# First attention: row-packed 48-row products for the softmax maxima, with the operand stacks laid out for two heads at once

## The chip, the cores and the metric

One core of a Trainium2 chip runs the whole program. The metric is the device time of one execution in microseconds (us). TensorE (PE) multiplies, VectorE (DVE) reduces and does elementwise work, ScalarE (ACT) does exponentials and copies, GpSimd (POOL) fills and gathers, SyncE (SP) issues DMAs.

## The reference, cut to what matters

A two-layer model over 8 images, each of 384 tokens (256 image rows and 128 text rows) with 256 channels. Only the first attention is touched. It has 16 heads of 16 channels and two sets of keys:

```
q, k, v, kp = heads(xn @ W_Q.T), heads(xn @ W_K.T), heads(xn @ W_V.T), heads(xn @ W_K_prime.T)
out = alpha * softmax(q k^T / 4) v + (1 - alpha) * softmax(q kp^T / 4) v
h = h + out @ W_O.T
```

## The kernel before, in words

`attention0` works image by image. An image's q, k and k' are projected in f32 and each is split into three bf16 parts (`parts`, L704 on ACT, L779, L782 and L784 on DVE), stored to a scratch array in HBM (L479) and read back as stacks of rows (L490): `qs` and `ks` hold, for each head, six blocks of 16 rows, one for each pair of parts in `SLOTS`, 96 rows in all (`NS`). A bf16 product of two stacks is then the sum of six part products. Four more rows in each stack carry the negated row maxima and the ones and zeros that switch them on for the right kind of key, so the scores that go to the exponential have 100 rows.

The 16 heads times 2 kinds of key are 32 units. While the units of image i are scored, the maxima of image i+1 are made:

- `scores` (L596): three matmuls for a unit into PSUM banks 4 to 6, then ACT's exponential over all three (L731). The next unit's scores wait for that exponential.
- `values` (L607): four matmuls of 128 rows by 32 columns, each in its own column quarter, in three of every four units (not in the first of a group of four).
- `ring`: three PSUM banks, one product of 128 x 384 in each (L584), reduced to a column of maxima by DVE (L795). An image has 96 products and, after each half of the heads, one transpose of the maxima (L581), which waits for all reduces so far. DVE negates and splits the maxima (L799, L802) and SP copies them as rows into `qs` (L499). `ring_part(v)` gives unit v three entries (four in two units).
- bank 3 serves one step in most units by the table `BANK3`: transposes of inputs (L545), outputs (L616) and y (L622), projections (L554, L562) and the output product (L630). A step waits until the step before it has been read out of the bank.

Each engine runs its own program in order. In a unit PE runs scores, values, ring entries, the bank-3 step. DVE runs the unit's reduces, then the unit's bank-3 work (three `low_parts` instructions for a projection, `normalize` for outputs, an addition). So a reduce of unit v+1 stands behind the bank-3 work of unit v.

Ahead of the loop lie two parts. A first block loads and transposes weights and makes layer-norm statistics. In the second block GpSimd fills the four switching rows of `ks` by four fills (L535, L538), while DVE normalizes image 0 (L768), PE and DVE make its parts, SP stores and stacks them. Then `first_ring` makes image 0's maxima, mixed with the projections of image 1, and the first scores follow.

SP's order in an image's turn: stacks of the next image's second half of heads, rows of maxima of its first half, the stores of the image after next, its first stacks, rows of maxima of the second half. A half's stacks are 18 DMAs, the maxima of a half 4.

## Time and profile before

| | |
|---|---|
| median of 3 runs | 2127.85 us (2125.75 to 2127.95) |
| the profiled execution | 2124.57 us, span 2122.70 us |
| attention0, first block | about 124.9 to 149.5 us |
| start to the first scores | about 150.0 to 280.8 us |
| the eight images' turns | about 280.8 to 915 us |

The profiled execution's time is 1.87 us over its span and 3.28 us under the median. In the rows below a time is in us from the start of the span unless it says ns, and a row of the timeline merges neighbouring instructions of one line.

### The profile page before, as it was taken

The numbers are of one execution on the slowest core, as the hardware profiler recorded it, in microseconds if no ns is written. First come the engines' busy times: TensorE is split into PE (matmuls) and PEld (weight loads), VectorE is DVE, ScalarE is ACT, GpSimd is POOL, SyncE is SP. The second block draws the span as 40 slices with busy tenths as digits, with TensorE's granted clock in tenths as the row PEclk, the third lists the DMA queues.
The fourth block names the chain that finished last, engine by engine and source line by source line (L and its number), as shares of the span: only waits on it lengthen the run. The fifth ranks groups of instructions, "written<-read, shape, count | busy, mean of one in ns | idle before, by whom it ended". The sixth has DMA issues, their size and how long they took to land. (4 is left out here: it accounts for less than half of the span.)

```text
span 2122.7 us, 29473 instructions
## 1 busy us (share of the span) xinstructions
PE 1828.5 (86%) x10095; PEld 1157.5 (55%) x10095; DVE 1102.2 (52%) x2272; ACT 667.6 (31%) x1032; POOL 352.9 (17%) x287
## 2 busy tenths in 40 slices
PE   5833698898898899758999589999989999999998
PEld 3521233433343343236666355666656676899997
DVE  6556778777787788147776454544332111222221
ACT  0111035564555555634444222323221111011110
POOL 0016000000000000017787021221102221100000
PEclk9876779999999999979999799999999999999999
DMA  4113824354364250010000470000001000334211
GB/s 150 52 47 58 110 34 80 67 58 69 55 82 68 35 96 8 1 46 0 0 0 0 155 253 1 0 0 0 1 1 37 30 25 22 114 140 151 94 36 33
DMA packets 112282, 117.25 MB, mean 55 GB/s; under 512 B 11453, under 2 KB 104127, under 8 KB 111936
## 3 DMA queue, kind: packets, MB, share of 16 engines
q1 hardware_dynamic: 99040, 87.73, 20.0%
q10 hardware_dynamic: 9504, 18.88, 2.5%
q0 software_dynamic: 3648, 9.46, 1.2%
q8 instruction: 54, 0.88, 0.2%
q14 instruction: 36, 0.29, 0.1%
HBM read 80.87 MB, written 35.29 MB: 55 GB/s over the span
## 5 line engine op out<-in xcount | busy, mean ns | idle before, releaser
L795 DVE TENSOR_REDUCE mx<-ps_a 128x1 f32<-128x384 f32 x768 | 375.5, 549 | 86.1 <-PE ps_a L584 83.9
L731 ACT ACTIVATE prob<-ps_a 128x1152 f32<-128x1152 f32 x256 | 289.4, 1130 | 216.0 <-PE ps_a L596 214.7
L584 PE MATMUL ps_a<-ks,qs 96*128 96x384 bf16 x768 | 197.7, 351 | 26.5 <-DMA ks<-parts_dram 17.0
L1820 PEld LDWEIGHTS ps_e<-xTr,w 128*128 128x128 f32 x1792 | 204.4, 192 | 2.2 <-issue 0.8
L1820 PE MATMUL ps_e<-xTr,w 128*128 128x128 f32 x1792 | 204.7, 275 | 0.6 <-DVE xTr L1993 0.6
L596 PE MATMUL ps_a<-qs,ks 100*128 100x384 bf16 x768 | 172.2, 333 | 24.2 <-ACT prob L731 19.8
L1756 PE MATMUL ps_e<-xT_all,w 128*128 (+1 forms) x512 | 169.7, 491 | 0.9 <-ACT xT_all L1847 0.9
L584 PEld LDWEIGHTS ps_a<-ks,qs 96*128 96x128 bf16 x768 | 62.4, 99 | 197.9 <-DVE mx L795 118.5
L607 PE MATMUL ps_a<-prob,vp 128*32 128x384 f32 x1536 | 165.5, 504 | 0.0
L1042 POOL TENSOR_TENSOR xb_f<-xb_f,xm_f 128x256 f32<-128x256 f32 x24 | 18.0, 752 | 755.7 <-ACT xm_f L1154 755.7
L1756 PEld LDWEIGHTS ps_e<-xT_all,w 128*128 128x128 f32 x512 | 97.5, 192 | 66.5 <-issue 1.8
L1090 PE MATMUL ps_f<-wguT,xT_f 128*128 128x352 f32 x384 | 123.2, 465 | 2.5 <-ACT xT_f L1135 2.5
L1883 ACT ACTIVATE gel_r<-ps_e 128x512 f32<-128x512 f32 x56 | 33.4, 597 | 279.9 <-PE ps_e L1820 279.9
L596 PEld LDWEIGHTS ps_a<-qs,ks 100*128 100x128 bf16 x768 | 64.2, 98 | 100.3 <-ACT prob L731 58.2
L1900 DVE TENSOR_TENSOR hid_e<-gel,ps_e 128x384 f32<-128x384 f32 x64 | 35.5, 554 | 136.0 <-ACT gel L1853 121.7
L1829 PE MATMUL ps_e<-w,hid_r 128*128 128x256 f32 x448 | 101.3, 379 | 0.0
L1462 PE MATMUL ps_a<-wsT,xT_a 128*128 128x512 f32 x192 | 88.8, 606 | 10.5 <-DVE lg L1364 10.0
L1853 ACT ACTIVATE gel<-ps_e 128x384 f32<-128x384 f32 x64 | 31.4, 490 | 207.3 <-PE ps_e L1756 207.3
L1090 PEld LDWEIGHTS ps_f<-wguT,xT_f 128*128 128x128 f32 x384 | 71.9, 193 | 36.1 <-ACT xT_f L1135 3.3
L2004 DVE TENSOR_TENSOR hid_r<-gel_r,ps_e 128x512 f32<-128x512 f32 x56 | 38.5, 687 | 100.4 <-ACT gel_r L1883 100.4
L1829 PEld LDWEIGHTS ps_e<-w,hid_r 128*128 128x128 f32 x448 | 82.9, 190 | 10.1
L554 PE MATMUL ps_a<-xT,wT 128*128 128x384 f32 x192 | 76.2, 524 | 14.0 <-DVE parts L784 12.6
(225 smaller groups left out, 2618.6 us busy)
## 6 DMA issues: line engine op xcount, KB each, us to landing
ks<-parts_dram SPq DMA_DIRECT2D x192, 96.0 KB, 6.4
w<-in_L_ffn_W_dram ACTq DMA_DIRECT2D x18, 1024.0 KB, 8.3
parts_dram<-parts SPq DMA_DIRECT2D x24, 576.0 KB, 3.7
qs<-parts_dram SPq DMA_DIRECT2D x96, 96.0 KB, 4.5
pix<-in_x_dram SPq DMA_DIRECT2D x24, 256.0 KB, 4.1
w<-in_L_ffn_W_dram SPq DMA_DIRECT2D x6, 1024.0 KB, 12.0
grouped_x<-empty_row SPq DMA_DIRECT2D x1, 4352.0 KB, 23.9
grouped_h<-empty_row SPq DMA_DIRECT2D x1, 4240.5 KB, 35.6
```

Source lines behind the costliest of these rows:

```text
L554: mm = pe.matmul(ps[:, bank, 0:T], wT[:, m, k, a * P:(a + 1) * P], xT[:, k], start=(k == 0), stop=(k == KC - 1))
L584: mm = pe.matmul(ps[:, r % 3, 0:T], qs[0:NS, b, u // 2, t * P:(t + 1) * P], ks[0:NS, b, u % 2, u // 2], start=True, stop=True)
L596: mm = pe.matmul(ps[:, 4 + t, 0:T], ks[0:NS + 4, b, kp, hh, t * P:(t + 1) * P], qs[0:NS + 4, b, hh], start=True, stop=True)
L607: mm = pe.matmul(ps[j * SLOT:(j + 1) * SLOT, 7, 0:T], vp[:, b, t, g // 2 * QUAD + j], prob[:, g % 2, j, t], start=(t == 0), stop=(t == TT ...
L731: act.activation(prob[:, g % 2, j], ps[:, 4:7, 0:T], ACT.Exp).then_inc(exp_done.sem, 1)
L795: dve.tensor_reduce(at, ps[:, r % 3, 0:T], AX.X, ALU.max).then_inc(ring_free.sem, 1)
L1090: mm = pe.matmul(ps[:, 2 * (u % 2) + n, 0:HALF0], xT[:, t, k], wguT[:, n, k, s * HALF0:(s + 1) * HALF0], start=(k == 0), stop=(k == KC - 1))
L1462: mm = pe.matmul(ps[:, n], xT[:, k, t * P:(t + 1) * P], wsT[:, k, n * 512:(n + 1) * 512], start=(k == 0), stop=(k == KC - 1))
L1756: mm = pe.matmul(ps[:, 2 * (a % 2) + m, 0:T], w12[:, 0, m, k, a * P:(a + 1) * P], xT_all[:, i, k], start=(k == 0), stop=(k == KC - 1))
L1820: mm = pe.matmul(ps[:, 2 * n + m, a * P:(a + 1) * P], w12[:, b, m, k, n * HALF1 + a * P:n * HALF1 + (a + 1) * P], xTr[:, k], start=(k == 0 ...
L1829: mm = pe.matmul(ps[:, 4, 0:C], hid_r[:, a], w3[:, b, a], start=(a == 0), stop=(a == IT1 - 1))
L2004: dve.tensor_tensor(hid_r[:, n * 4:(n + 1) * 4].rearrange("p a t -> p (a t)"), gel_r[:, n], ps[:, 2 * n + 1], ALU.mult).then_inc(rhid_done ...
```

## The change

1. The six part products are divided into `MAIN` (three) and `MINOR` (three). The products for the maxima use only the three main ones, 48 rows. The scores still use all six.
2. The stacks take all 128 rows. A head on side 0 has its main rows at 0 to 47 and its minor rows at 64 to 111, a head on side 1 the other way about. Heads 0 to 3 and 8 to 11 are on side 0, the others on side 1. The switching rows are 48 to 51 or 112 to 115. The scores take rows 0 to 111 or 0 to 115, with zeros between the blocks.
3. A ring item is now a pair: the same query tile and kind for one head of each side, at row offsets 0 and 64 of the array (`tile_position`), in two of the three banks. A pair waits until the item before the last entry is free, which for the second pair of a unit means that the first product of its first pair is reduced.
4. An image has 48 pairs and 2 transposes, 50 items, one or two in a unit (`ring_part`). The first item of a unit stands right behind its scores, ahead of `values`, the second behind `values`. DVE's order is as before: all reduces of a unit, then its bank-3 work. The first ring has two items (four reduces) for each projection step, where it had three reduces.
5. Stacks are one DMA for each block and side: 36 DMAs of 48 KB a half in place of 18 of 96 KB. Rows of maxima: 8 a half in place of 4.
6. The four fills of `ks` on GpSimd in the second block go. GpSimd now fills, in the first block, a small tile `ones` (four short fills) and zeros rows 32 to 63 of `qs` and `ks` as uint32 (6144 and 12288 elements a partition), and SP copies `ones` into the switching rows by 16 DMAs at the head of the second block.

```diff
-SLOTS = ((0, 0), (1, 0), (2, 0), (0, 1), (1, 1), (0, 2))
-NS = len(SLOTS) * D0
+MAIN = ((0, 0), (1, 0), (0, 1))
+MINOR = ((2, 0), (1, 1), (0, 2))
+NS = len(MAIN) * D0
+UPPER = P // 2
...
+    RING = [(q, kp, t) for q in range(QUAD) for kp in range(KINDS) for t in range(TT)] + [None]
+    NI = 2 * len(RING)
+    NT2 = 2 * len(RING) - 1
+    NR = 2 * NT2
     def ring_part(v):
-        return range(NR * v // UNITS, NR * (v + 1) // UNITS)
+        return list(range(NI * v // UNITS, NI * (v + 1) // UNITS))
+    def ring_item(e):
+        half, n = divmod(e, len(RING))
+        return half, n, half * NT2 + 2 * n
...
-    EARLY = 3
+    EARLY = 2
...
+            @block.gpsimd
+            def _(pool):
+                for kp in range(KINDS):
+                    pool.memset(ones[0:4, kp], float(kp)).then_inc(ones_made.sem, 1)
+                pool.wait_ge(ones_made.sem, 2)
+                for kp in range(KINDS):
+                    pool.memset(ones[0:2, kp], 1.0 - kp).then_inc(ones_made.sem, 1)
+                for stack in (qs[UPPER // 2:UPPER].rearrange("p b h t -> p (b h t)"),
+                              ks[UPPER // 2:UPPER].rearrange("p b k h t -> p (b k h t)")):
+                    pool.memset(stack.bitcast(U32), 0).then_inc(rows_zero.sem, 1)
...
-                        for s, pair in enumerate(SLOTS):
+                        for side in range(2):
+                            heads = quad(half, side)
+                            for pair, r in slot_rows(side):
...
+                for b in range(2):
+                    for kp in range(KINDS):
+                        for half in range(2):
+                            for side in range(2):
+                                r = shift_row(side, 0, 0)
+                                sp.dma_start(ks[r:r + 4, b, kp, quad(half, side)],
+                                             ones[:, kp].unsqueeze(1).to_broadcast([4, QUAD, T])).then_inc(ks_ready.sem, 16)
...
-            @block.gpsimd
-            def _(pool):
-                for kp in range(KINDS):
-                    pool.memset(ks[NS:NS + 4, :, kp], float(kp)).then_inc(ks_ready.sem, 1)
-                pool.wait_ge(ks_ready.sem, 2)
-                for kp in range(KINDS):
-                    pool.memset(ks[NS:NS + 2, :, kp], 1.0 - kp).then_inc(ks_ready.sem, 1)
...
+                        if r:
+                            pe.wait_ge(ring_free.sem, ring_free.at(i, r - 1))
...
+                        for side in range(2):
+                            hh, rows = (2 * half + side) * QUAD + q, main_rows(side)
+                            pe.matmul(ps[:, (r + side) % 3, 0:T], qs[rows, b, hh, t * P:(t + 1) * P],
+                                      ks[rows, b, kp, hh], start=True, stop=True, tile_position=(side * UPPER, 0)
+                                      ).then_inc(ring_full.sem, 1)
...
                         scores(i, b, v)
+                        if more:
+                            ring(i + 1, 1 - b, ring_part(v)[:1])
                         if j and g:
                             values(i, b, g - 1, j - 1)
...
                         if more:
-                            ring(i + 1, 1 - b, ring_part(v))
+                            ring(i + 1, 1 - b, ring_part(v)[1:])
```

## Rows read from the trace of the kernel before

**Rows 1.** The page, busy time and share of each engine.
```profile
PE 1828.5 (86%) x10095; PEld 1157.5 (55%) x10095; DVE 1102.2 (52%) x2272; ACT 667.6 (31%) x1032; POOL 352.9 (17%) x287
```
**Rows 2.** Windows: stretch, length, busy time by engine, granted clock, DMA share, GB/s.
```profile
181.40:218.30 36.90, 16.03 (x45) 9.29 (x45) 13.26 (x21) 5.33 (x11) 10.21 (x1) 0.69 0.63 102
218.30:280.70 62.40, 49.14 (x125) 15.44 (x126) 54.30 (x116) 4.70 (x8) 0.00 (x0) 0.69 0.58 82
615.50:698.10 82.60, 74.26 (x471) 32.09 (x471) 65.52 (x151) 44.76 (x52) 0.00 (x0) 1.00 0.44 66
```
**Rows 3.** Timeline of the second block's opening: start, length, instruction.
```profile
150.00 20.76 POOL L535 MEMSET ks<- 4x12288 bf16 x2 [146.73 <-POOLq L405]
150.04 31.29 DVE L768 TENSOR_SCALAR xn<-h,mv,rstd 128x256 f32<-128x256 f32 x3 [0.53 <-PEq L405]
...
187.57 4.25 DVE L782 CAST parts<-rest 128x384 bf16<-128x384 f32 x1
...
192.92 0.36 DVE L782 CAST parts<-rest 128x384 bf16<-128x384 f32 x1
...
199.61 1.05 DVE L768 TENSOR_SCALAR xn<-h,mv,rstd 128x256 f32<-128x256 f32 x3
```
**Rows 4.** Timeline of the first stacks and the first ring product.
```profile
200.12 3.62 SPq L490 DMA_DIRECT2D qs<-parts_dram  x6
203.78 5.63 SPq L490 DMA_DIRECT2D ks<-parts_dram  x12
...
218.35 1.12 PE L584 MATMUL ps_a<-ks,qs 96*128 96x384 bf16 x3 [17.02 <-DMA ks<-parts_dram]
...
218.87 3.09 DVE L795 TENSOR_REDUCE mx<-ps_a 128x1 f32<-128x384 f32 x6 [18.21 <-PE ps_a L584]
```
**Rows 5.** Timeline of the first block, DVE.
```profile
132.01 1.34 DVE L440 MEMSET vp<- 128x1536 f32 x1 [0.27 <-issue]
```
**Rows 6.** Timeline of one unit without a bank-3 step, PE, ACT and DVE.
```profile
514.67 0.66 PE L596 MATMUL ps_a<-qs,ks 100*128 100x384 bf16 x3
...
515.26 0.85 PE L607 MATMUL ps_a<-prob,vp 128*32 128x384 f32 x8
515.37 1.13 ACT L731 ACTIVATE prob<-ps_a 128x1152 f32<-128x1152 f32 x1 [0.76 <-PE ps_a L596]
...
516.05 0.66 PE L584 MATMUL ps_a<-ks,qs 96*128 96x384 bf16 x3
516.42 1.49 DVE L795 TENSOR_REDUCE mx<-ps_a 128x1 f32<-128x384 f32 x3 [0.40 <-PE ps_a L584]
...
516.56 0.66 PE L596 MATMUL ps_a<-qs,ks 100*128 100x384 bf16 x3
```
**Rows 7.** Timeline of units 14 and 15, a projection behind a projection.
```profile
651.86 0.56 DVE L784 TENSOR_TENSOR parts<-rest,parts 128x384 bf16<-128x384 f32 x1
652.34 1.48 DVE L795 TENSOR_REDUCE mx<-ps_a 128x1 f32<-128x384 f32 x3
...
652.48 1.56 PE L554 MATMUL ps_a<-xT,wT 128*128 128x384 f32 x4 [0.29 <-DVE parts L784]
...
653.87 0.65 PE L596 MATMUL ps_a<-qs,ks 100*128 100x384 bf16 x3
...
656.05 1.48 DVE L795 TENSOR_REDUCE mx<-ps_a 128x1 f32<-128x384 f32 x3
657.59 0.12 PEld L581 LDWEIGHTS ps_a<-ident,mx 128*96 128x96 f32 x1 [2.08 <-DVE mx L795]
```
**Rows 8.** Timeline of unit 1, DVE's outputs ahead of its reduces.
```profile
701.41 0.22 DVE L818 RECIPROCAL rec<-ps_a 128x12 f32<-128x12 f32 x1
...
701.93 0.36 DVE L824 TENSOR_TENSOR y<-ps_a,rec 128x192 f32<-128x192 f32 x1
```
**Rows 9.** Timeline, SP's stacks of a first half in a later turn.
```profile
501.25 3.43 SPq L490 DMA_DIRECT2D qs<-parts_dram  x6
...
504.72 7.22 SPq L490 DMA_DIRECT2D ks<-parts_dram  x12
```

More of the change, by code:

```diff
@@ L338, in attention0, with side_of, main_rows, slot_rows @@
     NM = HALF * TT
[L340 to L342 removed]
+    RING = [(q, kp, t) for q in range(QUAD) for kp in range(KINDS) for t in range(TT)] + [None]
+    NI = 2 * len(RING)
+    NT2 = 2 * len(RING) - 1
+    NR = 2 * NT2
     def ring_part(v):
[L346 removed]
+        return list(range(NI * v // UNITS, NI * (v + 1) // UNITS))
+    def ring_item(e):
+        half, n = divmod(e, len(RING))
+        return half, n, half * NT2 + 2 * n
+    def side_of(hh):
+        return hh // QUAD % 2
+    def main_rows(side):
+        return slice(side * UPPER, side * UPPER + NS)
+    def slot_rows(side):
+        for s in range(len(MAIN)):
+            yield MAIN[s], side * UPPER + s * D0
+            yield MINOR[s], (1 - side) * UPPER + s * D0
+    def shift_row(side, kp, k):
+        return side * UPPER + NS + 2 * kp + k
+    def all_rows(side):
+        return slice(0, UPPER + NS + 4 * side)
     BANK3 = {0: ("turn_outputs", 6), 3: ("values", 0), 4: ("turn_outputs", 7), 5: ("values", 1),
@@ L391, in attention0 @@
         mneg = sb("mneg", [P, 2, 2, P], BF16)
+        ones = sb("kind_rows", [4, KINDS, T], BF16)
         prob = sb("prob", [P, 2, QUAD, TT, T])
@@ L493, in maxima @@
                 def maxima(i, b, half):
                     sp.wait_ge(mneg_done.sem, mneg_done.at(i, half + 1))
+                    n = QUAD * TT
                     for kp in range(KINDS):
-                        for k in range(2):
-                            r = NS + 2 * kp + k
-                            n = NM // KINDS
-                            sp.dma_start(qs[r:r + 1, b, half * H0 // 2:(half + 1) * H0 // 2]
-                                         .rearrange("o h (a q) -> o (h a) q", q=P),
-                                         mneg[kp * n:(kp + 1) * n, half, k]).then_inc(mrow_in[half].sem, 16)
+                        for side in range(2):
+                            for k in range(2):
+                                r = shift_row(side, kp, k)
+                                sp.dma_start(qs[r:r + 1, b, quad(half, side)].rearrange("o h (a q) -> o (h a) q", q=P),
+                                             mneg[(2 * kp + side) * n:(2 * kp + side + 1) * n, half, k]
+                                             ).then_inc(mrow_in[half].sem, 16)
@@ L566, in ring @@
                 def ring(i, b, entries):
-                    for r in entries:
-                        u, t = RING[r]
-                        if r in (0, NR // 2):
+                    for e in entries:
+                        half, n, r = ring_item(e)
+                        if n == 0:
                             for m in range(3):
-                                signal = stack_in[r // (NR // 2)][m]
-                                pe.wait_ge(signal.sem, signal.at(i, 16 * len(SLOTS)))
-                        back = 3 if t is not None else 1
-                        if r >= back:
-                            pe.wait_ge(ring_free.sem, ring_free.at(i, r - back + 1))
+                                signal = stack_in[half][m]
+                                pe.wait_ge(signal.sem, signal.at(i, signal.per))
+                        if RING[n] is None:
+                            pe.wait_ge(ring_free.sem, ring_free.at(i, r))
+                            pe.transpose(ps[0:2 * NM, r % 3, 0:P], mx[:, half:half + 2].rearrange("p n k h t -> p (n k h t)"),
+                                         ident[:]).then_inc(ring_full.sem, 1)
+                            continue
+                        if r:
+                            pe.wait_ge(ring_free.sem, ring_free.at(i, r - 1))
@@ L586, in ring @@
-                        mm.then_inc(ring_full.sem, 1)
+                        q, kp, t = RING[n]
+                        for side in range(2):
+                            hh, rows = (2 * half + side) * QUAD + q, main_rows(side)
+                            pe.matmul(ps[:, (r + side) % 3, 0:T], qs[rows, b, hh, t * P:(t + 1) * P],
+                                      ks[rows, b, kp, hh], start=True, stop=True, tile_position=(side * UPPER, 0)
+                                      ).then_inc(ring_full.sem, 1)
```

62 lines of the change are left out of this document (30 added, 32 removed).

## The prediction

> **What bounds the kernel now.** I read the page first. PE is busy 86% of the span and no other engine over 52% [rows 1]. That is an average over five stages, so the share decides nothing here: the change touches the first attention alone, 124.9 to 915 us. I then took windows of its parts. From the start of image 0 (150 us) to the first stack products (218.3 us) hardly anything is computed. In the first ring (62.4 us) DVE is busy 54.3 us at a granted clock of 0.69, between TensorE's two levels. In a full turn of 82.6 us PE is modelled busy 74.3 us and DVE 65.5 us at clock 1.00, so neither is full [rows 2]. The timeline tells who waits. In the opening DVE needs 31.29 us for three normalizing instructions that take 1.05 us elsewhere, exactly while GpSimd runs its fills, and a cast takes 4.25 us in place of 0.36 [rows 3]. Then the first product waits 17.02 us for a DMA of the stacks [rows 4]. In the turns each unit is bounded by one of three things, and I looked at which one unit by unit.
>
> **The opening.** The change takes GpSimd's four fills out of the second block. The first normalization then ends 1.05 us after 150.04, that is at 151.1 in place of 181.3, a gain of 30.2 us [rows 3]. The cast's 3.9 us are given back too, but ahead of them PE was still making projections, and following the chain project, ACT, low parts by its own durations I get the last part 2.8 us earlier beyond the 30.2: 33.0 us in all.
>
> The fills now lie in the first block. The old fills do 12288 elements in 10.4 us, 0.85 ns an element [rows 3]; at this rate 6144 and 12288 uint32 take 5.2 and 10.4 us, and the small ones about 1.5 us. Started at 124.9 us they end near 142.5, ahead of the block's end at 149.5: cover by the layer-norm statistics on DVE, price nothing. What could be held there is DVE's fill of vp at 132.01 us. It takes 1.34 us for 1536 elements, 0.87 ns each [rows 5], as slow as GpSimd's, so it shows none of the double rate that the held instructions have (3 x 256 elements in 1.05 us with their fixed cost [rows 3]). I take 0; the upper end is one long fill, 10.4 us.
> The row shows DVE held by GpSimd for whole instructions, one normalization to each fill [rows 3]. The Trainium skill (SBUF — State Buffer, "Who interferes with whom") calls it an exclusive lock on a shared port pair that DVE's two-port modes take, and says that a DVE instruction with at most one SBUF input outside these modes doesn't contend. By that rule the fill of vp is not held and the price is 0, as taken.
>
> The 16 copies of `ones` are issued from 150 us on. A stack DMA costs SP 0.47 us (12 in 5.63 [rows 4]), so they are out by 158, and the first store isn't due before 160.8. They cost nothing.
>
> The stacks of the first half were 18 DMAs over 9.3 us and the last landed 8.9 us later, next to the second half's. Now they are 36 at 0.47 us plus the same 0.8 us of waits: 17.8 us, and they carry half the bytes each, so I let the last land in 4.5 us. That is 22.3 us against 18.2 [rows 4]: +4.1 us. Ends: 0 if the landing hides it, +9 if landing stays 8.9 us and the issue is slower.
>
> **The first ring.** It is DVE's: 96 reduces at 0.47 to 0.55 us [rows 2, 4]. Two effects. A projection step now has four reduces and a second pair that must wait for the first reduce behind `low_parts`: about 0.8 us more a step, six steps, less eight reduces (3.7 us) that are no longer due afterwards: +1 us. After that pairs alternate with three banks: a pair goes out when the reduce before the last is done, and at the low clock its result takes 0.55 us (product at 218.3, reduce at 218.87 [rows 4]) plus 0.05 of signal while DVE has only 0.47 us of work left. 32 pairs times 0.13 us: +4.3 us. At the high clock (0.42 us, product at 516.05 and reduce at 516.42 [rows 6]) it is 0; serial products would not add.
> Opening in sum: -33.0 + 4.1 + 1.0 + 4.3 = -23.6 us. Ends -33 and -5.
>
> **A turn.** Take the plain unit first. The next scores go 1.89 us after the last. ACT's exponential starts 0.70 us after the scores, lasts 1.13 and its signal takes 0.05: this loop sets the period [rows 6]. PE's own work in it: scores to values 0.59 us, values to ring 0.79, ring to scores 0.50, together 1.88, so PE has no slack either. A change of the array's tiling shows as follows: two products of one kind start 0.16 us apart, scores to values 0.25, so a change costs 0.09 us. The row-packed form isn't in the trace. I price each change of form by this nearest row, 0.09, and let the two products of a pair run side by side. Bounds: free changes (0), and a change that empties the array, a whole product of 0.33 plus a weight load of 0.10 instead of 0.25, 0.18 us dearer. The second product's bound is 0.16 us more (serial).
> The Trainium skill (TensorEngine Tiling (Array Packing), "Tiling Modes") says that changing the mode drains the engine. That speaks against this change, which adds one to two changes a unit. By the row between scores and values such a drain shows as 0.09 us; were it the whole length of the product, the upper bound would hold.
>
> A pair then takes 0.26 us of PE with its change. PE's work is 0.59 + 0.26 + 0.79 = 1.64 us with one item and 1.91 with two, plus the bank-3 step, against 1.88. With `ring_part` 14 units have one item and 18 have two (units 1, 3, 5, 7, 8, 10, 12, 14, 15, 17, 19, 21, 23, 24, 26, 28, 30, 31). Unit by unit:
> - One item, exponential the bound: 0. One item and PE the bound (6, 9, 11): -0.23 each, -0.69. Units 2 and 13, where reduces or outputs end last, -0.16 and -0.06. Sum -0.91.
> - Two items and PE the bound (3, 7, 10, 23, 26): +0.03 each, +0.15.
> - Two items where the second pair meets a busy DVE. It needs the first pair's first reduce, and this stands behind the bank-3 work of the unit before. In unit 14 the projection started at 652.48, just as `low_parts` of unit 13 ended at 652.42; all three ring products had found free banks. Now after 652.34 comes a reduce (0.55 with its end), a signal (0.05), the pair (0.26), and only then the projection, 0.7 us later or more: +0.76 [rows 7]. The projection, ACT and `low_parts` form the chain that sets these units (3.7 us each), so it isn't hidden. The same in 12 (+0.63) and 19 (+0.71).
> - Where `normalize` (0.9 us, 0.22 + 0.23 + 0.36 with gaps, or 1.25 with a second addition [rows 8]) stands ahead: unit 1, +0.75 (reduce from 701.85 in place of no wait), 5 +0.31, 17 +0.25, 21 +0.23. With the three above +3.64.
> - Two items without `values` to cover the first reduce (8, 24, 28) +0.29, +0.41, +0.26, and 30 behind them +0.20: +1.16.
> - The two transposes, which wait for all reduces. In unit 15 two reduces stand ahead in place of three (1.48 us [rows 7]): -0.47. In unit 31 the pair stands ahead of `values` and DVE is done 1.0 us earlier: -1.0. Sum -1.47.
> Turn: -0.91 + 0.15 + 3.64 + 1.16 - 1.47 = +2.57 us. DVE's work is the same 96 reduces. Five full turns +12.9. Image 0's turn has no outputs of a previous image: +1.7. Image 6's has no projections, so 12, 14, 17 and 19 go to +0.29, +0.03, +0.03, +0.03 and both transposes gain 1.0: +0.5. Image 7's has no ring: 0. The scores' 112 or 116 rows in place of 100 cost nothing: the products of 96 and 100 rows both take 0.66 us for three [rows 6]. Sum +15.1 us. Ends: -12 (the waits on reduces hidden, only the gains) and +60 (0.18 us on every change, some 40 that PE can't hide in a turn, and serial pairs).
>
> **SP.** A half's stacks cost 36 x 0.47 + 2.2 of waits = 19.2 us in place of 10.7 [rows 9]. The first half's begin 56.1 us into the turn, so they are issued at 77 with the delays above and landed at 82. The ring wants them at about 86. Hidden, with some 4 us to spare; without that cover each us goes to the turn. Second halves have 42 us. The 8 rows of maxima cost 3.1 us more behind a transpose that is due in the next turn or half: hidden.
>
> **Sum.** 2122.70 - 23.6 + 15.1 = 2114.2 us of span, 2116.1 for this execution with its 1.87 around the span. The runs' median is 3.3 above the execution's 2124.57, so I carry the difference of -8.5 to it: 2119.4 us, -0.40%.
>
> **Rivals.**
> - *Tiling changes are dear, slower.* At 0.18 us each in place of 0.09 some 44 changes a turn in units where PE or a two-item unit is the bound cost 4.0 us, over 6.4 turns +26: 2145 us. For it: the drain, and PE without slack. Against it: values show 0.09. It beats the opening from 0.12 us a change on. 20%.
> - *DVE's fill in the first block is held* for 10.4 us: 2130 us, no change. 12%.
> - *SP becomes the bound:* if a half-size DMA costs 0.78 us, the first half's stacks land at 92 us, 2.5 us late with six turns: 2134 us, slower. Against: the 0.47 us don't seem to come from the size. 10%.
> - *The waits for the reduces are hidden* and the gains stay: turns 0 to -1, 2103 us. For it: half of the units have reserve. Against: unit 14's chain. 16%.
> - My forecast 42%.
> Under 0.2% (4.3 us) a measurement can't tell. Faster: the forecast nearly all (0.40) and the hidden waits (0.16): 0.56. Same: the held fill and the forecast's edge, 0.16. Slower: 0.28. The range leaves out the dear changes' upper half and little of the hidden waits: 2101 to 2143. The forecast's own range is 2112 to 2126.
>
> **What would show it.** `xn` at 150 takes about 1 us, and the first stack product comes near 189 us (a fill of vp at 132 over 1.5 us shows the second rival). First scores near 257. Plain one-item units keep 1.88 us, two-item units 1.91; unit 14 grows from 3.72 to 4.5 and unit 31 falls from 3.5 to 2.5; scores to pair starts 0.25 apart, pair to values 0.25 (0.35 shows the first rival). The prediction is wrong if turns grow by over 4 us or shrink.

## The result and the profile after

The changed kernel takes 2136.44 us (median of 7 runs, 2133.06 to 2139.34) against 2127.95 us for the kernel before in the same comparison (7 runs, 2125.75 to 2129.0). The ratio is 1.004 with a 95% interval of 1.003 to 1.005: 0.4% slower, where 0.4% faster was forecast. The time lies inside the range of 2101 to 2143 us, on the wrong side of no change. The profiled execution took 2139.32 us, 2137.5 of span, at the upper end of its runs, so the two traces differ by 14.8 us where the medians differ by 8.5.

First the page of the changed kernel: busy time and share of each engine, and the granted clock in 40 slices.
```profile
PE 1814.2 (85%) x10095; PEld 1133.5 (53%) x10095; DVE 1079.1 (50%) x2272; ACT 671.6 (31%) x1032; POOL 328.4 (15%) x289
...
PEclk9876589999899999989999799999999999999999
```
Against [rows 1] PE, DVE and POOL are each less busy, and the kernel is slower. The totals can't say why; the stages can. Next, windows of the changed kernel: the opening up to the first ring product, the first ring, and the turn of image 4. The columns are those of [rows 2].
```profile
151.20:187.70 36.50, 15.05 (x45) 9.41 (x46) 10.52 (x24) 5.33 (x11) 0.00 (x0) 0.69 0.37 105
187.70:266.30 78.60, 41.19 (x125) 12.62 (x126) 57.88 (x116) 4.70 (x8) 0.00 (x0) 0.54 0.24 67
620.30:707.10 86.80, 73.41 (x472) 29.16 (x472) 66.54 (x151) 45.34 (x52) 0.00 (x0) 0.98 0.23 63
```
The first ring was 62.4 us long at a granted clock of 0.69 [rows 2]; now it is 78.6 us at 0.54, close to the lower of the two levels (1.2 GHz) all along, though the number of instructions is the same. The turn grew by 4.2 us. Summed by stage, in the profiled executions:

| | before | after | difference | forecast |
|---|---|---|---|---|
| the second block's first normalization starts | 150.04 | 151.28 | +1.2 | 0 |
| first ring product | 218.35 | 187.71 | -30.6 | -28.9 |
| first ring product to first scores | 62.41 | 78.67 | +16.3 | +5.3 |
| eight turns | 629.8 | 656.8 | +27.0 | +15.1 |
| all behind the first attention's turns | 1212.2 | 1214.4 | +2.2 | 0 |
| span | 2122.7 | 2137.5 | +14.8 | -8.5 |

(The first row is contained in the second.) The opening came as forecast. This is the changed kernel's timeline of it:
```profile
132.75 10.33 POOL L458 MEMSET ks<- 32x12288 uint32 x1
...
133.25 1.34 DVE L485 MEMSET vp<- 128x1536 f32 x1 [0.27 <-issue]
...
151.28 1.06 DVE L822 TENSOR_SCALAR xn<-h,mv,rstd 128x256 f32<-128x256 f32 x3 [0.53 <-PEq L435]
...
168.10 6.66 SPq L539 DMA_DIRECT2D qs<-parts_dram  x12
174.82 11.20 SPq L539 DMA_DIRECT2D ks<-parts_dram  x24
...
187.71 0.50 PE L635 MATMUL ps_a<-ks,qs 48*128 48x384 bf16 x2 [18.40 <-DMA ks<-parts_dram]
```
The normalization that took 31.29 us [rows 3] takes 1.06. The 36 stack DMAs are issued in 17.9 us, and the product goes 1.7 us behind the last issue. DVE's fill of `vp` takes 1.34 us while GpSimd's long fill runs beside it, exactly what it took alone [rows 5].

Now the first ring of the changed kernel, PE alone, from the timeline:
```profile
215.12 2.93 PE L602 MATMUL ps_a<-xT,wT 128*128 128x384 f32 x4
217.98 0.50 PE L635 MATMUL ps_a<-ks,qs 48*128 48x384 bf16 x2
220.67 0.50 PE L635 MATMUL ps_a<-ks,qs 48*128 48x384 bf16 x2 [2.19 <-DVE mx L849]
221.10 2.93 PE L602 MATMUL ps_a<-xT,wT 128*128 128x384 f32 x4
...
228.80 0.50 PE L635 MATMUL ps_a<-ks,qs 48*128 48x384 bf16 x2 [0.65 <-DVE mx L849]
229.95 0.50 PE L635 MATMUL ps_a<-ks,qs 48*128 48x384 bf16 x2 [0.65 <-DVE mx L849]
```
Beside it two projections of the kernel before, in the same stage and at the high level of the clock:
```profile
225.70 1.56 PE L554 MATMUL ps_a<-xT,wT 128*128 128x384 f32 x4 [1.67 <-DVE parts L784]
...
229.42 1.56 PE L554 MATMUL ps_a<-xT,wT 128*128 128x384 f32 x4 [1.67 <-DVE parts L784]
```
Read three things. A projection takes 2.93 us in place of 1.56. A step, from one projection to the next, takes 5.98 us; in the kernel before it took 3.72. And PE waits 2.19 us of each step, now for a reduce; before it waited 1.67 us, for `low_parts`. Behind the steps a pair goes every 1.15 us.

Last, units 12 to 14 of image 4's turn in the changed kernel, from the timeline. `L648` are scores, `L635` a pair, `L668` transposes of outputs, `L602` a projection, `L838` the last `low_parts` instruction.
```profile
651.44 0.56 DVE L838 TENSOR_TENSOR parts<-rest,parts 128x384 bf16<-128x384 f32 x1
651.91 2.00 DVE L849 TENSOR_REDUCE mx<-ps_a 128x1 f32<-128x384 f32 x4
...
652.52 0.34 PE L635 MATMUL ps_a<-ks,qs 48*128 48x384 bf16 x2 [2.04 <-DVE mx L849]
...
652.79 0.55 PE L668 MATMUL ps_a<-ident,osb 128*128 128x128 f32 x3
...
653.17 0.65 PE L648 MATMUL ps_a<-qs,ks 116*128 116x384 bf16 x3
...
655.25 2.76 PE L602 MATMUL ps_a<-xT,wT 128*128 128x384 f32 x4
...
657.85 0.65 PE L648 MATMUL ps_a<-qs,ks 116*128 116x384 bf16 x3
...
659.56 0.56 DVE L838 TENSOR_TENSOR parts<-rest,parts 128x384 bf16<-128x384 f32 x1
660.03 2.00 DVE L849 TENSOR_REDUCE mx<-ps_a 128x1 f32<-128x384 f32 x4
...
660.64 0.34 PE L635 MATMUL ps_a<-ks,qs 48*128 48x384 bf16 x2 [1.09 <-DVE mx L849]
...
660.91 1.56 PE L602 MATMUL ps_a<-xT,wT 128*128 128x384 f32 x4
...
662.30 0.65 PE L648 MATMUL ps_a<-qs,ks 116*128 116x384 bf16 x3
```
At 660.64 stands the wait that was forecast for unit 14. `low_parts` ends at 660.12, one reduce follows, the second pair goes at 660.64 and the projection at 660.91, 0.79 us behind `low_parts`; in [rows 7] it was 0.06. The same wait in unit 12 (at 652.52) leaves PE idle for 2.04 us, and the next projection, in unit 13, then runs at 1.2 GHz: 2.76 us and a unit of 4.68 us. That second effect wasn't in the forecast. It doesn't follow each such wait: in the turns of images 1, 3, 4 and 5 unit 13 takes 4.56 to 4.67 us, in those of images 0 and 2 it takes 3.39 and 3.38, behind the same wait (2.04 us, 1.87 in images 0 and 5).

The turns nearly whole, in the view of PE's waits from 266 to 900 us (us in all, times, longest):
```profile
PE ps_a L635 <- DVE mx L849: 43.8, 50, 2.0
PE ps_a L648 <- ACT prob L785: 22.0, 61, 0.9
PE ps_a L624 <- DVE mx L849: 13.1, 15, 1.6
```
In the kernel before, ring products waited 0.3 us for reduces in all turns together, the transposes of the maxima 20.2 us (14 times), the scores 19.8 us for ACT. Over the changed kernel's whole turns, to 923 us and without the first ring's last transpose, the three are 43.8, 11.9 (14 times) and 27.2 us. The transposes' wait fell by 8.3 us, in the direction that was forecast; the pairs' new one of 43.8 stands against it, and the scores wait 7.4 us more for ACT. No product waits for a DMA.

Unit by unit: median time from one unit's scores to the next's, over the turns of images 1 to 5:

| unit | before | after | difference | forecast |
|---|---|---|---|---|
| 1 | 1.99 | 2.88 | +0.89 | +0.75 |
| 9 | 2.20 | 2.07 | -0.13 | -0.23 |
| 12 | 2.95 | 3.61 | +0.66 | +0.63 |
| 13 | 3.53 | 4.56 | +1.03 | -0.06 |
| 14 | 3.72 | 4.46 | +0.74 | +0.76 |
| 19 | 4.15 | 4.89 | +0.74 | +0.71 |
| 28 | 1.91 | 2.23 | +0.32 | +0.26 |
| 31 | 3.48 | 2.38 | -1.10 | -1.0 |
| sum of all 32 | 82.33 | 86.61 | +4.28 | +2.57 |

Unit 13 alone makes up 1.09 of the 1.71 us that the sum is off.

### The profile page after: what moved, and what is told of

The parts are those of the page before. It is cut to its first block and busy times, and to the rows that moved or that the text cites. A ratio compares the mean times of both kernels' runs of the same rounds, so it can differ in the third digit from the quotient of the medians.

```text
span 2137.5 us, 29665 instructions
## 1 busy us (share of the span) xinstructions
PE 1814.2 (85%) x10095; PEld 1133.5 (53%) x10095; DVE 1079.1 (50%) x2272; ACT 671.6 (31%) x1032; POOL 328.4 (15%) x289
## 5 line engine op out<-in xcount | busy, mean ns | idle before, releaser
L849 DVE TENSOR_REDUCE mx<-ps_a 128x1 f32<-128x384 f32 x768 | 388.1, 552 | 88.5 <-PE ps_a L635 81.8
L635 PE MATMUL ps_a<-ks,qs 48*128 48x384 bf16 x768 | 139.4, 360 | 101.8 <-DVE mx L849 79.0
L648 PE MATMUL ps_a<-qs,ks 112*128 112x384 bf16 (+1 forms) x768 | 173.0, 335 | 32.0 <-ACT prob L785 27.2
L635 PEld LDWEIGHTS ps_a<-ks,qs 48*128 48x128 bf16 x768 | 37.4, 94 | 264.6 <-DVE mx L849 204.0
L648 PEld LDWEIGHTS ps_a<-qs,ks 112*128 112x128 bf16 (+1 forms) x768 | 65.2, 99 | 123.3 <-ACT prob L785 80.0
L602 PE MATMUL ps_a<-xT,wT 128*128 128x384 f32 x192 | 87.4, 590 | 4.9 <-DVE parts L838 3.7
```

Of the source, the lines that this page charges most:

```text
L602: mm = pe.matmul(ps[:, bank, 0:T], wT[:, m, k, a * P:(a + 1) * P], xT[:, k], start=(k == 0), stop=(k == KC - 1))
L635: pe.matmul(ps[:, (r + side) % 3, 0:T], qs[rows, b, hh, t * P:(t + 1) * P], ks[rows, b, kp, hh], start=True, stop=True, tile_position=(sid ...
L648: mm = pe.matmul(ps[:, 4 + t, 0:T], ks[rows, b, kp, hh, t * P:(t + 1) * P], qs[rows, b, hh], start=True, stop=True)
L849: dve.tensor_reduce(mx[:, half, kp, side * QUAD + q, t:t + 1], ps[:, (r + side) % 3, 0:T], AX.X, ALU.max).then_inc(ring_free.sem, 1)
```

## The experiments

Ten kernels ran. All times are medians, and each ratio is against the kernel before with its 95% interval. "First ring" is the time from the first ring product to the first scores, "turns" the sum of the eight. The kernel before has 62.4 and 629.8 us, the changed one 78.7 and 656.8. These stage times, and the units, are those of one profiled execution of each kernel.

**1. The opening alone.** The kernel before with the small tile `ones` filled in the first block and copied into the switching rows by four DMAs; its stacks and its ring are untouched.
```diff
+            @block.gpsimd
+            def _(pool):
+                for kp in range(KINDS):
+                    pool.memset(ones[0:4, kp], float(kp)).then_inc(ones_made.sem, 1)
...
+                for b in range(2):
+                    for kp in range(KINDS):
+                        sp.dma_start(ks[NS:NS + 4, b, kp],
+                                     ones[:, kp].unsqueeze(1).to_broadcast([4, H0, T])).then_inc(ks_ready.sem, 16)
...
-                for kp in range(KINDS):
-                    pool.memset(ks[NS:NS + 4, :, kp], float(kp)).then_inc(ks_ready.sem, 1)
```


> The kernel before with one edit: the switching rows of ks are filled once into a small tile in the first block and copied by 4 DMAs, so GpSimd fills nothing beside the first normalization. Ring, stacks, scores as before. If the hold of VectorE by GpSimd's fills is a delay of its own: normalization 1.06 us in place of 31.3, first ring product near 218.3 - 33 = 185 us, first ring and turns as before (62 and 629 us), in all -33 us: 2095 us, ratio 0.985. Rival, the delay is given back later since the DMAs or the low clock of the first ring take it: ring product late or first ring over 70 us, a ratio over 0.99.

Measured: 2093.4 us (4 runs, 2092.61 to 2095.84), ratio 0.984 (0.9823 to 0.9858), 34.4 us less than the runs of the kernel before beside it (2127.77). Its windows, opening and first ring:
```profile
151.20:185.00 33.80, 14.83 (x45) 9.03 (x43) 9.47 (x21) 5.34 (x11) 0.00 (x0) 0.70 0.74 117
185.00:246.90 61.90, 48.78 (x125) 15.28 (x126) 54.31 (x116) 4.71 (x8) 0.00 (x0) 0.69 0.58 83
```
The first product goes at 185.07 us, 33.3 earlier than before; ring (61.8) and turns (629.6) are those of the kernel before. So the opening's gain belongs to the fills alone, and the rest of the change costs 43 us (2136.44 against 2093.4). It is the fastest kernel of the study.

**2. The second pair behind the bank-3 step.** The changed kernel; if the wait for the first reduce costs because the projection is queued behind it, it should go when the projection goes first.
```diff
-                        if more:
-                            ring(i + 1, 1 - b, ring_part(v)[1:])
                         step, n, of = bank3(v, prev, more, more2)
                         if step:
                             last = in_bank3(step, i + of, n, last)
+                        if more:
+                            ring(i + 1, 1 - b, ring_part(v)[1:])
```


> The changed kernel with a unit's second item behind the bank-3 step in TensorE's order, so that projections, output products and transposes no longer stand behind the wait for the first pair's first reduce. The first ring is left. If that wait is what lengthens the turns: units 12, 14 and 19 fall from 3.61, 4.45 and 4.89 us to about 3.0, 3.75 and 4.2, unit 13 from 4.56 to 3.4 as the clock no longer falls in it, a full turn from 88 to about 84 us, over six turns -22 us: ratio to the kernel before near 0.993. Rival, the form change of the array and the two-item units are what costs: the long units fall but others grow as much, the turn stays over 87 us, ratio 1.00 or more.

Measured: 2133.64 us (6 runs, 2127.53 to 2136.36), ratio 1.0027 (1.001 to 1.0044); turns 654.9. Units 12, 14 and 19 fell as meant, to 3.31, 4.08 and 4.52, but the next scores now stood behind the waiting pair: units 9, 16, 18, 20 and 30 grew to 2.45, 3.16, 4.03, 2.23 and 2.24, and the medians of the 32 units sum to 86.9 us against 86.6. The wait moved and didn't go. The slow projection moved too: unit 13 fell to 3.77, but unit 17, 3.40 in the changed kernel, takes 4.93 to 5.04 us in the turns of images 1 to 3, at the low clock, and that alone is 1.5 us of the sum. So this run doesn't tell what the new order is worth with the clock held up.

**3. A busy first ring.** The changed kernel with PE kept working in its first ring: products into bank 4, which nobody reads there, four between the two pairs of a projection step, and one between the pairs behind the steps. It leaves nothing out.
```diff
+                def busy(count):
+                    for _ in range(count):
+                        pe.matmul(ps[:, 4, 0:C], wT[:, 0, 0, 0:P], wT[:, 0, 1, 0:C], start=True, stop=True)
...
-                    ring(0, 0, entries)
+                    ring(0, 0, entries, (4, 1) if step == "project" else ())
```


> The changed kernel with products of constants into an unused bank put where TensorE waits between the items of the first ring (four in a projection step, one between items behind them). It adds work only. If the low granted clock is what makes the first ring 78.7 us in place of the 67.7 forecast: the clock of the stretch rises to near 1, a projection takes 1.5 us in place of 2.9 and a pair's period falls from 1.15 to 1.0 us, first ring about 66 us, -12 us against the changed kernel, ratio to the kernel before near 0.998. Rival, the ring's length comes from the order of waits alone: the clock rises and the ring stays at 76 us or more, or grows by the added work.

Measured: 2119.36 us (5 runs, 2118.33 to 2122.8), ratio 0.9968 (0.9953 to 0.9983). Window of the first ring, then PE's timeline in it (`L617` are the added products):
```profile
188.50:255.30 66.80, 61.63 (x241) 29.33 (x242) 56.68 (x116) 4.70 (x8) 0.00 (x0) 0.93 0.29 80
```
```profile
203.11 0.34 PE L642 MATMUL ps_a<-ks,qs 48*128 48x384 bf16 x2 [0.44 <-DVE mx L856]
...
205.14 1.99 PE L617 MATMUL ps_a<-wT 128*128 128x256 f32 x8
...
207.57 0.34 PE L642 MATMUL ps_a<-ks,qs 48*128 48x384 bf16 x2 [0.44 <-DVE mx L856]
...
207.84 1.56 PE L602 MATMUL ps_a<-xT,wT 128*128 128x384 f32 x4
```
The ring falls from 78.7 to 66.8 us at clock 0.93 with more work in it, the projection is back at 1.56 us, a step takes 4.46 us in place of 5.98, and pairs go every 0.98 us in place of 1.15. The forecast had 67.7 for this stage. So 11.9 of the first ring's 16.3 us are the clock.

The turns fell as well, to 648.6 us in place of 656.8, though nothing was added in them: 23.9 us of them are at the low clock in place of 46.6. Unit 13 takes 3.39 us in the turns of images 1, 2, 4 and 5 (4.15 in 3, 4.56 in 0), behind the same wait of the second pair in unit 12. Here that wait and the projection behind it, in image 4's turn:
```profile
635.77 0.34 PE L642 MATMUL ps_a<-ks,qs 48*128 48x384 bf16 x2 [2.04 <-DVE mx L856]
...
638.42 1.56 PE L602 MATMUL ps_a<-xT,wT 128*128 128x384 f32 x4 [0.29 <-DVE y L891]
```
So the wait in unit 12 doesn't by itself bring the low clock to unit 13. Whether the busy ring kept it away or the stretches at the low clock merely fell elsewhere isn't shown.

**4. Single entries.** The changed kernel's layout and packed form, but the two products of a pair as two entries of their own, each waiting only for the bank three entries back, three or four in a unit behind `values`, as before.
```diff
-    RING = [(q, kp, t) for q in range(QUAD) for kp in range(KINDS) for t in range(TT)] + [None]
+    RING = [(q, kp, t, side) for q in range(QUAD) for kp in range(KINDS) for t in range(TT) for side in range(2)] + [None]
...
-                        if r:
-                            pe.wait_ge(ring_free.sem, ring_free.at(i, r - 1))
+                        if r >= 3:
+                            pe.wait_ge(ring_free.sem, ring_free.at(i, r - 2))
```


> The changed kernel with its stacks, rows and row-packed form, but the ring in single entries as in the kernel before: three or four a unit, all behind values, each waiting for the bank of three entries earlier, three a step in the first ring; neighbouring entries lie in the two halves of the array's rows. If the grain of a pair (two banks of three, one or two pairs a unit) is the fault and the packed form is cheap: units 12, 14, 19 at 2.95, 3.75 and 4.15 us, a full turn of 82 to 83 us as in the kernel before, first ring near 62 us, ratio 0.985 like the opening alone. Rival, the form changes cost more than the 0.09 us they were priced at, or 48-row products let the clock fall: turn of 85 us or more, ratio 0.995 or more.

Measured: 2107.7 us (4 runs, 2106.26 to 2109.16), ratio 0.9907 (0.989 to 0.9923); turns 636.5; units 12, 14 and 19 at 2.95, 3.72 and 4.15, exactly as before. Window of its first ring:
```profile
187.20:254.10 66.90, 55.17 (x125) 15.16 (x126) 54.33 (x116) 4.71 (x8) 0.00 (x0) 0.55 0.29 79
```
It runs at the low clock (0.55) and yet takes 66.9 us. Against experiment 1's 61.8 us at 0.69 the packed form with its low clock costs 5.1 us here; the pairs with the clock held up cost 5.0 (experiment 3); both together, in the changed kernel, 16.8. So most of the loss needs both: take the low clock away and 11.9 us go, take the pair's wait away (this one) and 11.8 go. Behind the steps the third bank hides the slower product with single entries; with pairs, product, two reduces and signal stand in one chain. The run shows one thing more: the clock is as low without any wait of a pair, so it doesn't take those waits to hold it down.

In the turns the coarser grain of the pairs, with their place ahead of `values`, costs 656.8 - 636.5 = 20.3 us, the packed form and the layout 636.5 - 629.6 = 6.9 us. The stretches at the low clock are contained in both (46.6 us of the turns in the changed kernel, 34.4 here, 23.9 in experiment 1).

**5. Busy turns.** The changed kernel with three or four added products in units 12, 13, 14, 16, 18 and 19, into the free ring bank, as soon as the item before has been reduced.
```diff
+                BUSY = {12: 4, 13: 3, 14: 3, 16: 4, 18: 4, 19: 3}
...
+                        pe.wait_ge(ring_free.sem, ring_free.at(i, r))
+                        for _ in range(BUSY[v]):
+                            pe.matmul(ps[:, (r + 2) % 3, 0:C], wT[:, 0, 0, 0:P], wT[:, 0, 1, 0:C], start=True, stop=True)
```


> The changed kernel with three or four products of constants, written to a free ring bank, where TensorE waits in units 12, 13, 14, 16, 18 and 19 of the turns of images 1 to 6. The wait of the second pair stays. If the low clock in the turns is a second cost on top of the waits: unit 13 falls from 4.56 to 3.4 us in every turn, unit 17 never reads 4.89, and the turns of images 1 to 5 fall from 86.6 in the median to about 85.4 us and from 438.1 in sum to about 429. Rival, the slow units 13 and 17 come from the wait alone: they stay, and the turns grow by the added work.

Measured: 2152.08 us (4 runs, 2147.26 to 2154.64), ratio 1.0119 (1.0102 to 1.0137); turns 668.9. The granted clock is the high one throughout images 1, 2, 4, 5 and 6, so the added work does keep it up, but it lies on the path itself (units 16 and 18 at 3.01 and 4.75 in place of 2.78 and 3.72). It can't tell what the clock is worth; experiment 8 asks with fewer products.

**6. Both items behind `values`.** The changed kernel's pairs in the old place.
```diff
                         scores(i, b, v)
-                        if more:
-                            ring(i + 1, 1 - b, ring_part(v)[:1])
...
-                            ring(i + 1, 1 - b, ring_part(v)[1:])
+                            ring(i + 1, 1 - b, ring_part(v))
```


> The changed kernel with the first item of a unit behind values too. By the bank rule the second pair then waits for a reduce that has only begun: a two-item unit with values takes 0.59 + 0.79 + 0.26 and, behind the first pair's 0.37 of latency and 0.60 of reduce, another 0.26 from there, about 2.7 us in place of 1.91, for some 7 plain units of this kind and 0.3 to 0.7 us in others: turn of 91 us or more, ratio over 1.02. If the grain of a pair were not what costs, the turn would stay near 87 us, since TensorE does the same work with a form change less.

Measured: 2193.7 us (4 runs, 2192.5 to 2196.47), ratio 1.0309 (1.0292 to 1.0326); turns 715.7. A plain unit with two items takes 2.63 us in place of 1.91: the second pair waits for the first's reduce with nothing between them. Putting the first pair ahead of `values` is worth 58.9 us, part of it by the clock (74.5 us of the turns at the low clock here, 46.6 in the changed kernel); it is what makes the pairs bearable.

**7. Three of the six terms alone.** Experiment 1 with its products for the maxima over 48 rows, neither packed nor paired, with no other stacks. The maxima come from three of the six part products, as in the change.
```diff
-SLOTS = ((0, 0), (1, 0), (2, 0), (0, 1), (1, 1), (0, 2))
+SLOTS = ((0, 0), (1, 0), (0, 1), (2, 0), (1, 1), (0, 2))
...
-                            mm = pe.matmul(ps[:, r % 3, 0:T], qs[0:NS, b, u // 2, t * P:(t + 1) * P],
-                                           ks[0:NS, b, u % 2, u // 2], start=True, stop=True)
+                            mm = pe.matmul(ps[:, r % 3, 0:T], qs[0:NMAIN, b, u // 2, t * P:(t + 1) * P],
+                                           ks[0:NMAIN, b, u % 2, u // 2], start=True, stop=True)
```


> The kernel of the first experiment (opening alone) with the three main blocks first in its stacks and the products for the maxima over these 48 rows only, unpacked. If a product's time goes by its columns, fewer rows buy nothing: products 0.16 us apart, turns 629.6 us in sum as without, ratio to the kernel before 0.984 as there. Rival, fewer active rows lower the clock or let the products run shorter: low clock in more of the turns and a ratio over 0.988, or turns under 627 us.

Measured: 2151.04 us (4 runs, 2149.88 to 2152.33), ratio 1.0113 (1.0096 to 1.0129); turns 682.2 in place of 629.6, for products that take the same 0.66 us for three. PE's timeline of one unit without a bank-3 step (`L604` scores, `L615` values, `L592` ring products):
```profile
821.23 0.66 PE L604 MATMUL ps_a<-qs,ks 100*128 100x384 bf16 x3
821.82 0.85 PE L615 MATMUL ps_a<-prob,vp 128*32 128x384 f32 x8
822.60 0.66 PE L592 MATMUL ps_a<-ks,qs 48*128 48x384 bf16 x3
823.19 0.66 PE L604 MATMUL ps_a<-qs,ks 100*128 100x384 bf16 x3
```
The unit takes 1.96 us in place of 1.89. From the last ring product to the scores it is 0.26 us, where two products of 96 and 100 rows are 0.16 apart: ring to scores now costs what a change of form does, though nothing is packed. Besides, 17 to 21 us are at 1.2 GHz in five of the eight turns, where experiment 1 has 0 to 10: 110.8 us in all against 23.9.

**8. A busy first ring and one busy unit.** Experiment 3, and four added products in unit 12 alone, where PE would wait 2.04 us.
```diff
+                        if more and prev and v == 12:
+                            busy(i + 1, 4)
                         if more:
                             ring(i + 1, 1 - b, ring_part(v)[1:])
```


> The changed kernel with added products of constants in the first ring (as in the third experiment) and four more in unit 12 alone, whose second pair leaves TensorE idle for 2.04 us and after which the clock fell. The products fit into that wait. If the low clock in unit 13 comes from the idle time in unit 12: unit 12 stays near 3.6 us, unit 13 at 3.4 us in all turns (it read 4.56 in four of six), the turns of images 1 to 5 sum to about 430 us against 438.1, ratio near 0.995, a little under the third experiment's 0.9968. Rival, the low stretches only move to other units: unit 13 at 3.4 but the sum stays over 436.

Measured: 2118.18 us (9 runs, 2116.61 to 2119.84), ratio 0.9962 (0.9951 to 0.9973). PE's timeline of units 12 and 13, where `L619` are the added products:
```profile
629.63 0.65 PE L662 MATMUL ps_a<-qs,ks 116*128 116x384 bf16 x3
...
630.49 1.99 PE L619 MATMUL ps_a<-wT 128*128 128x256 f32 x8
632.60 0.34 PE L649 MATMUL ps_a<-ks,qs 48*128 48x384 bf16 x2
...
633.25 0.65 PE L662 MATMUL ps_a<-qs,ks 116*128 116x384 bf16 x3
...
635.24 1.56 PE L602 MATMUL ps_a<-xT,wT 128*128 128x384 f32 x4 [0.28 <-DVE y L900]
636.63 0.65 PE L662 MATMUL ps_a<-qs,ks 116*128 116x384 bf16 x3
```
Unit 12 keeps its 3.61 us, the projection in unit 13 is at 1.56, and unit 13 takes 3.38 us in images 1 to 5. All turns together take 648.4 us, 8.4 less than in the changed kernel. But experiment 3, with nothing added in unit 12, has 648.6 us and 3.39 in unit 13 in four of these five turns. The comparison that isolates the four products is with experiment 3, and it gives 0.2 us in the turns and 1.2 in the medians. So this run doesn't show that the idle time in unit 12 brought the low clock to unit 13. What the two runs show together is what fewer stretches at the low clock are worth in the turns: 8.2 and 8.4 us, with 23.9 and 20.5 us at the low clock in place of 46.6.

**9. Ring ahead of `values`, without pairs.** Experiment 1 with its single products right behind the scores, the transposes where they were.
```diff
                         scores(i, b, v)
+                        if more and v != HALF:
+                            ring(i + 1, 1 - b, [r for r in ring_part(v) if RING[r][1] is not None])
```


> The kernel of the first experiment with the ring's products (three single entries, 96 rows, not packed) ahead of values in a unit, the transposes of the maxima left behind values. The number of form changes stays. VectorE gets its reduces about 0.8 us earlier. Unit 31, where the transpose waits for the unit's reduces, falls from 3.48 to about 2.8 us, unit 1 and 2 by 0.1 together, the others stay: -0.7 us a turn and in image 6's unit 15 too, about -5 us: ratio 0.982 against 0.984. Rival, the products wait for banks and hold up values, so units grow: 0.985 or more.

Measured: 2097.22 us (4 runs, 2096.03 to 2101.52), ratio 0.9874 (0.9851 to 0.9897); turns 635.9. Unit 31 falls to 2.59 us (2.38 in the changed kernel), but unit 1 rises to 2.86 and unit 30 to 2.28: behind `normalize` the reduces are late whatever the form of the products. So unit 1's +0.89 and 0.89 of unit 31's -1.10 in the changed kernel come from the order, and the order alone gains nothing: the turns are 6.3 us longer than in experiment 1.

**10. Five of the six terms alone.** Experiment 7 with 80 rows, so that the maxima come from five of the six part products.
```diff
-NMAIN = 3 * D0
+NMAIN = 5 * D0
```


> As the three-term experiment, but the products for the maxima over five of the six blocks, 80 rows. With 48 rows two things came together: a form change on each side of the ring's products (0.255 us between starts in place of 0.16) and 17 us of low clock in most turns. Over 64 rows the form is that of the full array. If the form change and what it leaves idle is the cause, 80 rows behave as 96: turns 630 us in sum, ratio 0.984. If the clock answers to the rows in use, low clock of several us remains in the turns and the ratio is over 0.988.

Measured: 2099.87 us (4 runs, 2095.61 to 2101.46), ratio 0.9882 (0.9861 to 0.9904). The medians of the units sum to 82.5 us, experiment 1's to 82.3, and all turns take 632.5. So the 52.6 us that 48 rows cost in experiment 7 come nearly all between 80 and 48 rows, with the change of form and the longer stretches at the low clock; these two weren't separated. What remains to experiment 1 (2.9 us in the eight turns, 1.0 in the first ring) lies in stretches at the low clock, 29.5 us of the turns in place of 24. The medians are 6.5 us apart; the profiled execution was the fastest of its four, so it doesn't show all of this. Why the stretches at the low clock are longer with fewer rows in use isn't settled.

## Why the prediction was wrong

**The opening was right.** Forecast -28.9 us to the first product, measured -30.6, or -31.9 counted from the normalization, which now starts 1.2 us later. Experiment 1 shows the part of the fills by itself: -33.3, forecast -33.0. The stacks' +4.1 was +2.6 (187.71 against 185.07), and only +1.1 counted from the normalization, which starts at 149.70 us in experiment 1. The fill in the first block cost nothing: DVE's 1.34 us stood unchanged beside it, so the rival of a held fill is refuted. (The prediction's reason, a double rate of the held instructions, doesn't come out of its row: 3 x 256 elements in 1.05 us are 1.37 ns an element with their fixed cost, not under the fill's 0.87.) The Trainium skill (SBUF — State Buffer, "Who interferes with whom") says that such an instruction doesn't contend; the trace agrees, 1.34 us alone and beside the fill.

**The step that failed is "about 0.8 us more a step, six steps ... +1 us" in the first ring**, together with what the same omission did in the turns. It sets 0.8 us on top of the step of before, 3.72 + 0.8 = 4.5 us, and so takes over that step's projection of 1.56 us. In experiment 3, with the clock held up, a step takes 4.46 us and the whole ring 66.8 (forecast 67.7): the wait was priced rightly. In the changed kernel a step takes 5.7 to 6.0 us, because the granted clock falls from 0.69 to 0.54 and the projection in the step's chain takes 2.9 us. Why the clock falls is shown in part. Added work lifts it (experiment 3). It doesn't take the pairs' waits, since it is 0.55 with single entries too (experiment 4). It goes with the products over 48 rows: 0.63 where they are neither packed nor paired (experiment 7), 0.66 over 80 rows (experiment 10), 0.69 over 96 (experiment 1). What in the packed form brings it down to 0.55 stays open. The +4.3 for the pairs had been priced at the low clock and was nearly right (1.15 us a pair against 1.07). The forecast took the clock that the stage had before as given, though the change takes work from PE in it. The term was +5.3 us and measured +16.3; experiment 3 takes 11.9 of it away.

**The turns' list of waits was right, and the same omission stands beside it.** Units 12, 14 and 19 grew by 0.66, 0.74 and 0.74 against 0.63, 0.76 and 0.71; units 1, 28 and 31 came as forecast. Units of one or two items that PE bounds lost or gained up to 0.1 us more than forecast. Unit 13 (+1.03 against -0.06) and unit 17 at times (4.89 in images 0 and 3) ran their projection at 1.2 GHz, and the forecast held no such term. Experiments 3 and 8 take 8.2 and 8.4 us of the turns' 27.0 away and leave +18.8 and +18.6 against the +15.1 forecast. Much of the other 3.5 us is image 0's turn, 7.6 us longer than before in the changed kernel against +1.7 forecast; it starts at the low clock (22.7 us of it, 10.8 before), and with experiment 8's busy ring ahead of it still 4.6 longer. What starts a stretch at the low clock in one turn and not in the next, behind the same wait, stays open.

In experiment 3 both losses by the clock are gone, 11.9 + 8.2 = 20.1 us of the 23.3 by which the changed kernel's span missed the forecast one (2137.5 against 2114.2). Its median is 2119.36 us, and the forecast was 2119.4. That these agree so closely is luck: its span is 3.4 us over the forecast one, with the turns 3.7 longer and the part behind them 1.4.

**The rivals.** Dear changes of tiling, 20%: refuted. Scores to pair starts 0.26 us apart and pair to values 0.26, as in this stretch of PE's timeline in the changed kernel (0.35 would have shown the rival):
```profile
856.49 0.65 PE L648 MATMUL ps_a<-qs,ks 116*128 116x384 bf16 x3
857.08 0.34 PE L635 MATMUL ps_a<-ks,qs 48*128 48x384 bf16 x2
857.34 0.85 PE L659 MATMUL ps_a<-prob,vp 128*32 128x384 f32 x8
858.37 0.34 PE L648 MATMUL ps_a<-qs,ks 116*128 116x384 bf16 x1 [0.17 <-ACT prob L785]
```
The Trainium skill (TensorEngine Tiling (Array Packing), "Tiling Modes") says that a change of mode drains the engine; in this trace a change of form costs 0.09 to 0.10 us, 0.26 from start to start in place of 0.16. The rival got the sign right, for another reason. SP as the bound: refuted, a stack DMA of half the size costs 0.50 us to issue in the opening (36 in 17.9), and no product of the turns waits for a DMA. Hidden waits: refuted, by the units above. None of the rivals held the one thing that decided, the clock. It had no chance of its own, and so "slower" had 0.28.

**Where the gain went.** The opening saves 32 to 33 us and keeps them. Against experiment 1, the pairs' grain and order take back 20.3 us in the turns and 11.8 in the first ring (experiment 4; what the low clock adds with pairs is contained in both). The packed form and layout take back 6.9 and 5.1 us, again with the clock's part in them. The layout's extra DMAs take 1.1 to 2.6 us. PE's shorter work gains only where PE is the bound, 0.13 to 0.18 us in units 6, 9 and 11; elsewhere ACT or a wait sets the unit.

## What to carry to other kernels

Before adding up an edit that takes work from TensorE or adds waits to it, redo the price of every projection or long product that stands in a chain at 1.2 GHz, and give "the clock falls" a chance of its own: here that term (20 us) was larger than the sum's own result (8.5 us), and a row for it was in the trace of before (the projection at 220.87 us, mostly at the low clock, took 2.68 us in place of 1.56). Packing two products into one slot saves array time and makes the buffer coarser: with three banks pairs leave no spare bank, so each pair waits for a whole reduce; count the banks, and put other work between two packed items. When one change holds two independent edits, run each alone: here one gained 34.4 us and the other lost 43. And compare a filler with the kernel that differs by that filler alone: against the changed kernel experiment 8's four products seemed to gain 1.3 us in unit 13, against experiment 3 they gain nothing there.

## What the hardware did that was not expected

- Two products in the two halves of the array's rows start 3 ns apart and take 0.34 us together, hardly more than one (0.33). PE's time is saved; in most units nothing was waiting for it.
- A product over 48 rows, with no position in the array given, behaves as another form than one over 96 or 100: next to those it starts 0.26 us behind in place of 0.16 (experiment 7). At 80 rows there is no such step: 0.16 and 0.17 us (experiment 10).
- Added work made a stage faster: PE is modelled busy for 41.2 us in a first ring of 78.6 us at a granted clock of 0.54, and for 61.6 us in one of 66.8 at 0.93.
- The same wait of 2.04 us in unit 12 is followed by a projection of 2.76 us at the low clock in image 4's turn of the changed kernel and by one of 1.56 us in experiment 3.
- GpSimd's uint32 fills take 0.84 ns an element a partition (12288 in 10.33 us), about what its bf16 fills took (12288 in 10.38). The bf16 fills held DVE's normalizations [rows 3]; the uint32 fill beside DVE's own fill of `vp` didn't hold it.
